# A two-layer Mamba/attention kernel on one core: unshifted write vectors moved through DRAM rows, score maxima turned on VectorE, and a newly searched instruction order

## The chip, the cores and the metric

The kernel runs on one core of a Trainium2 chip as one launch. The time is the device time of that core in microseconds, taken as the median of three runs. The engines are called by the profile's names: PE (TensorE), DVE (VectorE), ACT (ScalarE), POOL (GpSimd) and SP (SyncE, which issues nearly all the DMAs here).

## The reference, cut to what matters

`x` is 8 batches of 1024 tokens of 256 channels. Layer 0 is a selective scan with its feed-forward block and an MLP. Layer 1, the one whose computation the change touches, normalises `x` and adds an attention with a "line memory" and a second MLP:

```python
qkv = (x @ qkv_w + qkv_b).reshape(Bx, Tx, 3, H, DH)      # 16 heads of 16
attn = softmax(causal scores);  seq_out = attn @ v
x_prev = jnp.concatenate([jnp.zeros((Bx, 1, Dx)), x[:, :-1]], axis=1)
w1 = (x_prev @ w1_write).reshape(Bx, Tx, H, PD)           # PD = 4: 64 columns, of the token before
w2 = (x @ w2_write).reshape(Bx, Tx, H, PD)
write_lines, read_lines = exterior(w1, w2), exterior(x @ w1_read, x @ w2_read)
mem_score = sum over earlier tokens of decay**distance * (read_line . J write_line)**2
gated = mean over heads of sigmoid(mem_score * mem_scale) * sigmoid(x @ memg_w + memg_b)
out = (seq_out + gated * (x @ memv_w + memv_b)) @ out_w + out_b
```

The softmax needs the maximum of every row of scores. `w1` is a projection of the token before: row t of it is row t-1 of `x @ w1_write`, and row 0 is zero.

## The kernel before, in words

**Order.** The order of every engine's work is written at build time by a planner (`by_time`, fed by `layer0_tasks` and `layer1_tasks`). It knows for every task the engine (p = PE, a = ACT, v = DVE, g = POOL, s = SP), a length, a tick (when it is wanted), what must come before it, and how late its result is felt; it then takes tasks by time. `SHIFTS` moves the ticks of a kind of task, `DRIFT` and `PULL` weigh ticks against readiness, and `ACTIVE`, `WINDOW`, `LOW` are its model of PE's clock. Each engine runs its list strictly in order, so a wait holds all that is behind it on its engine. PSUM banks are given out by the same planner: pairs of banks for scores ("wide"), single banks for the rest ("dense").

**Layer 0** takes the first half of the span. PE adds scanned states and runs the projections, DVE scans, POOL forms the scans' inputs, and SP feeds broadcast rows.

**Layer 1** works batch by batch, 8 pairs of heads in each batch, 64 pairs in all. In a pair g:
- `sm` units (L1539): PE makes scores in nine pieces, DVE takes their row maxima into `smax` (L2131, L2134, L2138), 8 tiles of 128 rows for both heads.
- `mt` (L1547): one PE transpose of the 16 columns of `smax` into a dense bank, so that each row of 128 maxima lies in one partition. ACT writes the negated high part (`neg_hi`), DVE the rest (L2141, `neg_lo`).
- `maxima` on SP (L1343): two DMAs put them as extra rows of `qs`. Then the `st` units (L1557) make the transposed scores with the maximum already taken off, ACT exponentiates them, POOL masks the crossing tiles, `pv` (L1576) multiplies with the values, and `ot` (L1584) turns the result.

Once in a batch the dense work runs between the pairs: `xt` turns the normalised input into `xT`, `qk` (L1610) projects queries and keys, and for each of 8 token tiles there are
- `pa` (L1616): six matmuls of 464 columns (values, w1_read, w2_write, w2_read, the gate);
- `pb` (L1621 and L1624): six matmuls of 256 columns for `memv_w`, and six of 64 columns for `w1_write`, the latter with the weights side taken from `xT` one token earlier. `xT` has a leading column of zeros for that (the `zeros` task on DVE). ACT copies the 64 columns into `pt1[:, t % 4, 0:64]`.

As soon as a tile's `pb` is drained, POOL forms its outer products (`outer`, L2431) and DVE the lines (L2221). For each half batch of four tiles a chain follows: `square`, `length`, `unit`, `lt`, `jw`, `feat_r` and `feat_w` on POOL (L1166), `fw` and `fr` (L1642), scans on DVE, and `ms` (L1648). After the second `ms` of a batch SP may load the MLP's weights (L1290, L1293) over the buffers that the chain used. `e1` (L1668) and `e2` (L1673) add a rank-one term to these weights, then `f1` (L1681) and `o` (L1689), the MLP, can run, and the next batch's `pa` waits for its last `o`.

`pt1` and `pt2` hold four tiles, `outer` two. The `pa` of a tile is drained only when the `outer` of four tiles earlier is done.

Of the kernel before, what the change touches and what calls it, by code (L numbers as in the profile page):

```python
# [12 lines left out]
F32 = mybir.dt.float32  # L13
F32R = mybir.dt.float32r
BF16 = mybir.dt.bfloat16
ALU = mybir.AluOpType
# [3 lines left out]
P = 128  # L20
B, S, D = 8, 1024, 256
NT = S // P
# [429 lines left out]
LENGTH = {"xt": 0.44, "qk": 1.40, "pa": 1.28, "pb": 1.40, "lt": 0.44, "jw": 0.89, "fw": 0.44, "fr": 0.44, "ms": 0.44,  # L452
# [20 lines left out]
def layer1_tasks():  # L473
# [37 lines left out]
    def pair(g):  # L511

        b, first = g // NG, g * TICKS
        for n, unit in enumerate(MAX_UNITS):
# [3 lines left out]
                + (0.26 if n == len(MAX_UNITS) - 1 else 0), tick, ("p", "sm", g, n))  # L518
        place["mt", g] = first + TICKS - LEAD
        add("p", ("mt", g), 0.11, place["mt", g], ("v", "sm", g, len(MAX_UNITS) - 1))  # L520
        add("a", ("mt", g), EMPTY_A["mt"], place["mt", g], ("p", "mt", g), ("s", "maxima", g - 1) if g else None)
        add("v", ("mt", g), EMPTY_V["mt"], place["mt", g], ("a", "mt", g))
        add("s", ("maxima", g), 1.2, place["mt", g], ("v", "mt", g), late=2.0)
# [32 lines left out]
    for b in range(B):  # L556
# [19 lines left out]
        for c in range(NC):  # L576
            for t in range(TC * c, TC * (c + 1)):
# [3 lines left out]
                      a=[("g", "outer", (n - TC) // NT, (n - TC) % NT)] if n >= TC else [])  # L581
                dense(("pb", b, t), ("p", "pa", b, t))
                add("g", ("outer", b, t), 1.05, place["pb", b, t], ("a", "pb", b, t),
# [44 lines left out]
    for g in range(PAIRS):  # L628
# [7 lines left out]
          "pb": 0.62, "f1": 0.92}  # L636
# [14 lines left out]
def at_pace(used, start, length, active):  # L651

    now = start
    while length > 1e-9:
# [11 lines left out]
TURN, DRIFT = 0.1, 0.042  # L666
SHORT, RUN, STAY = 0, 1, 0
PULL = {"a": 0.01, "v": 0, "g": 0.01, "s": 0.0}
SHIFTS = {
    ("a", 0): {"xt": -23, "yt": 4, "res": 24, "skip": 19, "decay": 5, "gelu": 18, "dl": 8, "soft": 13, "cv": 1,  # L670
        "norm": 5.5, "m": -7, "silu_x": -9, "h": -10, "centre": -17, "o": -1, "shift": -2, "square": 8},
    ("a", 1): {"logistic": 56, "length": 41, "turn": -13, "deviation": 29, "f1": -26},
    ("g", 0): {"drive": 6, "du": 26, "join": 8, "offset": -15},
    ("g", 1): {"feat_r": 7, "select": 21},
# [5 lines left out]
    ("v", 0): {"scan": 44, "weigh": -49, "stats": 33.4},  # L680
    ("v", 1): {"gate": 34, "e2": 17, "wo": -6, "bias": 36, "pa": -2.4, "fw": 8, "stats": 7, "xt": 14, "lines": 59,
        "normal": 30, "zeros": 25, "sm": 3, "ot": -3},
}

# [6 lines left out]
def shift_of(name):  # L691

    attention = name[1] == "L1"
    return SHIFTS.get((name[0], int(attention)), {}).get(name[2] if attention else name[1], 0.0)
# [134 lines left out]
def pool_of(unit):  # L829

    if unit[0] != "L1":
        return "side" if unit[0] in LENGTH0 else None
    return "wide" if unit[1] in ("sm", "st", "ot") else "dense" if unit[1] in LENGTH or unit[1] == "mt" else None
# [24 lines left out]
def build(nc, x_in, w_in, p_in, moe1_in, moe2_in, resid, out):  # L858
    ctx = ExitStack()
    with ctx:  # L860
# [24 lines left out]
        def param(name):  # L885
# [33 lines left out]
        (qs, ks, exps, vals0, z0, parts, oT, rden, total, smax, smax2, gate_in, mem_in, gate8, l1_at) = place(  # L919
            arena_at, ("qs", [P, SLOTS, S], F32R), ("ks", [P, SLOTS, S], F32R), ("exps", [P, RING_COLS]),  # L920
            ("vals0", [P, vals_cols]), ("z0", [P, NT, D]), ("parts", [P, 2, 2, HALF], F32R), ("oT", [P, S]),
            ("rden", [P, NT, 2]), ("total", [P, NT, 2, VC1]), ("smax", [P, H, NT]), ("smax2", [P, 2, NT - TC, NC]),
# [253 lines left out]
        def _(sp):  # L1176
# [99 lines left out]
            def attention_task(task):  # L1276
# [62 lines left out]
                elif kind == "maxima":  # L1339
                    for who in "av":  # L1340
                        drained(sp, plan, ("mt", n), who)
# [1201 lines left out]
```

## Time and profile before

| | us |
|---|---|
| runs | 3705.8, 3708.39, 3709.55 |
| median | 3708.39 |
| the profiled execution's own time | 3712.95 |
| its span, first to last instruction | 3711.2 |
| PE busy | 3545.9 (96%) |
| DVE busy | 3105.8 (84%) |
| ACT busy | 2681.1 (72%) |
| POOL busy | 2286.7 (62%) |
| granted TensorE clock, mean | 0.985 |

Busy time is the union of an engine's instructions. PE's matmuls overlap, so for PE the distance between starts tells more than the duration of one. A granted clock of 1 is 2.4 GHz, and 0.5 is 1.2 GHz.

### The profile page before, as it was taken

Reading aid. Unit: us, or ns where it says so; the run is one execution under the profiler, and the core shown is the slowest. Engines: PE = TensorE matmul, PEld = TensorE weight load, DVE = VectorE, ACT = ScalarE, POOL = GpSimd, SP = SyncE. Lnnn points to the kernel's source line nnn. Section 1 sums busy time; section 2 is a strip of 40 time slices with the busy share of each in tenths; the row PEclk is TensorE's granted clock in tenths of the full one; section 3 lists DMA queues with packets and bytes.
Section 4 is the critical chain, followed back from the end, with each engine's and each line's share of the span. In section 5 each row is a group of like instructions: output and inputs, shape, how many; then the busy total and the mean of one; then the engine's idle time right before and its main releaser. Section 6 shows DMA issues by size and latency. Waiting matters only on the chain.

```text
span 3711.2 us, 63758 instructions
## 1 busy us (share of the span) xinstructions
PE 3545.9 (96%) x20578; PEld 2371.7 (64%) x20578; DVE 3105.8 (84%) x5827; ACT 2681.1 (72%) x4174; POOL 2286.7 (62%) x1799
## 2 busy tenths in 40 slices
PE   8999999999999999999897999999999999999998
PEld 4666666666666665666664766666666666767665
DVE  4788999999999999999957697786968778696873
ACT  7768878888888888888635667576675757667565
POOL 4787989999999999999914152331514233251421
PEclk9999999999999999999997999999999999999998
DMA  4445545455555555555523223232412323241230
GB/s 172 139 149 167 164 149 183 154 176 171 177 162 160 182 160 178 168 175 161 185 78 95 62 67 88 70 119 62 127 54 67 96 70 119 62 127 46 75 85 21
DMA packets 253342, 456.90 MB, mean 123 GB/s; under 512 B 26116, under 2 KB 80852, under 8 KB 250196
## 3 DMA queue, kind: packets, MB, share of 16 engines
q1 hardware_dynamic: 253012, 452.82, 39.5%
q8 instruction: 168, 2.75, 0.3%
q14 instruction: 162, 1.33, 0.1%
HBM read 381.07 MB, written 69.21 MB: 121 GB/s over the span
## 4 chain that ended last, share of the span: by engine, by line
PE 31%; DVE 12%; issue 4%; ACT 2%; POOL 1%; DMA 1%; SPq 0%; DVEq 0%; POOLq 0%; ACTq 0%
PE ps L1689 6%; PE ps L1576 4%; PE ps L1681 4%; PE ps L1557 3%; PE ps L1539 3%; DVE ps L2131 2%; DVE smax L2134 2%; PE ps L1610 2%; PE ps L1616 2%; PE ps L1621 1%; PE ps L1584 1%; ACT exps L1706 1%; DVE lines L2221 1%; PE ps L1624 1%; DMA g<-in_weights 1%
## 5 line engine op out<-in xcount | busy, mean ns | idle before, releaser
L2371 POOL TENSOR_TENSOR drive<-du,b_wide 128x1024 f32<-128x1024 f32 x512 | 1198.8, 2367 | 33.4 <-DVE ps L2108 24.5
L1706 ACT ACTIVATE ps<-delta,neg_a 128x512 f32<-128x512 f32 x1024 | 682.6, 685 | 145.4 <-DVE heavy L2086 109.1
L1706 ACT ACTIVATE exps<-ps 128x1024 f32<-128x1024 f32 (+1 forms) x640 | 598.7, 938 | 217.8 <-PE ps L1557 213.2
L2405 POOL TENSOR_SCALAR_AFFINE_SELECT exps<-exps 128x256 f32<-128x256 f32 x512 | 210.0, 424 | 798.0 <-ACT exps L1706 797.9
L2131 DVE CUSTOM_DVE_ANT_0 ps<-ps,later 128x512 f32<-128x512 f32 (+3 forms) x1024 | 474.6, 518 | 68.5 <-PE ps L1539 66.8
L1491 PEld LDWEIGHTS ps<-p_all,heavy 128*128 128x128 f32 x3072 | 352.9, 141 | 175.3 <-issue 84.1
L2086 DVE TENSOR_TENSOR heavy<-c_wide,ps 128x512 f32<-128x512 f32 x704 | 449.3, 674 | 11.8 <-issue 8.1
L2108 DVE TENSOR_TENSOR_SCAN ps<-ps,carry,drive 128x512 f32<-128x512 f32 x352 | 434.7, 1274 | 16.7 <-ACT ps L1706 15.3
L1491 PE MATMUL ps<-p_all,heavy 128*128 128x128 f32 x3072 | 413.7, 276 | 35.9 <-DVE heavy L2086 23.3
L2108 DVE TENSOR_TENSOR_SCAN ps<-ps,drive 128x512 f32<-128x512 f32 x352 | 413.2, 1213 | 31.9 <-ACT ps L1706 25.2
L2353 POOL TENSOR_TENSOR held<-held,c_wide 128x1024 f32<-128x1024 f32 x160 | 377.4, 2359 | 44.7 <-DVE held L2108 37.2
L2134 DVE TENSOR_REDUCE smax<-ps 128x2 f32<-128x1024 f32 x256 | 311.9, 1219 | 66.8 <-PE ps L1539 66.1
L1706 ACT ACT_TABLE_LOAD x277 | 355.4, 1283 | 5.7 <-PEq L2536 0.8
L1576 PE MATMUL ps<-exps,vals 128*32 128x512 f32 (+3 forms) x3072 | 306.6, 502 | 17.2 <-POOL exps L2405 8.0
L1557 PE MATMUL ps<-qs,ks 64*128 64x512 f32 (+3 forms) x1536 | 291.4, 405 | 11.8 <-DVE mem_in L2262 3.6
L1706 ACT ACTIVATE h<-ps,p_all 128x256 f32<-128x256 f32 (+1 forms) x384 | 193.8, 539 | 126.1 <-PE ps L1681 92.0
L1539 PE MATMUL ps<-ks,qs 64*128 64x512 f32 (+3 forms) x1536 | 262.3, 379 | 15.2 <-ACT exps L1706 10.9
L1427 PE MATMUL ps<-mT,w_up 128*128 128x512 f32 x512 | 244.7, 601 | 11.1 <-ACT h L1706 6.3
L1557 PEld LDWEIGHTS ps<-qs,ks 64*128 64x128 f32 x1536 | 137.0, 187 | 170.0 <-issue 78.2
L1689 PE MATMUL ps<-g,h 128*128 128x256 f32 x1024 | 236.0, 383 | 0.0
L1437 PE MATMUL ps<-w_down,h 128*128 128x256 f32 x1024 | 234.1, 382 | 0.0
L2108 DVE TENSOR_TENSOR_SCAN held<-ps,drive 128x512 f32<-128x512 f32 x160 | 189.7, 1208 | 49.9 <-POOL drive L2371 37.3
(219 smaller groups left out, 7151.4 us busy)
## 6 DMA issues: line engine op xcount, KB each, us to landing
b_wide<-bc_dram SPq DMA_DIRECT2D x512, 256.0 KB, 3.6
c_wide<-bc_dram SPq DMA_DIRECT2D x512, 256.0 KB, 3.6
stacks<-parts SPq DMA_DIRECT2D x192, 256.0 KB, 2.6
qs<-stacks SPq DMA_DIRECT2D x128, 192.0 KB
ks<-stacks SPq DMA_DIRECT2D x128, 192.0 KB, 4.3
x_row<-in_x SPq DMA_DIRECT2D x14, 1024.0 KB, 8.1
resid<-mix SPq DMA_DIRECT2D x9, 1024.0 KB, 5.4
x_row<-resid SPq DMA_DIRECT2D x9, 1024.0 KB, 5.5
```

The costliest lines, as they stand in the source:

```text
L1491: last = mm(acc_tile(t)[:, d * P:(d + 1) * P], heavy[:, slot, t * P:(t + 1) * P], ident, is_transpose=True, start=(u == 0 and d == 0 and t ...
L1539: last = mm(both[:, i * HALF + off:i * HALF + off + n], qs[head, slot, it * P:(it + 1) * P], ks[head, slot, ch * HALF:ch * HALF + n], star ...
L1557: last = mm(both[:, i * HALF + off:i * HALF + off + n], ks[head, slot, jt * P:(jt + 1) * P], qs[head, slot, at:at + n], start=True, stop=T ...
L1576: last = mm(ps[tile:tile + VP, PV_BANK, HALF - n:], vals[b % 2][:, first:first + VP], exps[:, at + i * apart + off:at + i * apart + off + ...
L1689: last = mm(bank[:, 0:D], h1[:, q % 2, m, tt * P:(tt + 1) * P], g2[:, m, :], start=(m == 0), stop=(m == MF - 1))
L1706: return nc.scalar.activation(out_, in_, func, **kw)
L2086: V.tensor_tensor(heavy[:, piece % W_SLOTS, :], c_wide[:, g % C_SLOTS, :], state_bank(k), ALU.mult).then_inc(weighed, 1)
L2108: V.tensor_tensor_scan(into, state_bank(k), drive[:, g % DRIVE_SLOTS, d, :], carry[:, e, n, d:d + 1] if j % NC else 0.0, ALU.mult, ALU.add ...
L2131: last = V.tensor_tensor_reduce(part[:, i, :], part[:, i, :], later[:, HALF - n:], 1.0, -3.0e38, ALU.add, ALU.max, into[:, i, :])
L2134: last = V.tensor_reduce(into[:, :, 0], part, AX_X, ALU.max)
L2353: G.tensor_tensor(states, states, wide(c_wide[:, g % C_SLOTS, :], MD), ALU.mult)\
L2371: G.tensor_tensor(drive[:, g % DRIVE_SLOTS, :, :], du[:, e, :, :], wide(b_wide[:, g % B_SLOTS, :], MD), ALU.mult).then_inc(driven, 1)
```

## The change

1. `pb` becomes six matmuls of 320 columns on the unshifted tokens. ACT copies the 64 columns into a new buffer `ahead` (8 tiles). When four tiles are there, SP writes them to rows 1 + token of a DRAM tensor `ahead_rows` (`put`: 128 partitions by 4 tiles, 256 bytes each), and then reads the rows one earlier back into `pt1` (`shift`: the same shape). Row 0 of each batch is set to zero once. `outer` waits for `shift`; all four of a half are released together.
2. `mt` leaves PE. `smax` becomes two slots of 32 columns (16 used, zeroed once on POOL); DVE turns one slot with four 32x32 transposes into `turned` (`flip`), ACT and DVE read `turned` instead of a PSUM bank.
3. The two memsets of `xT`'s leading columns go.
4. The planner's costs and edges follow, `DRIFT`, `PULL` and all of `SHIFTS` (layer 0's too) are new, and single units of `sm`, `st`, `pv` get shifts of their own (`UNIT_SHIFTS`). `LOW`, the edge of the planner's clock rule, has the same value in both files.

```diff
-"pb": 1.40
+"pb": 0.92
-        add("p", ("mt", g), 0.11, place["mt", g], ("v", "sm", g, len(MAX_UNITS) - 1))
+        add("v", ("flip", g), 0.42, at, ("v", "sm", g, len(MAX_UNITS) - 1), ("v", "mt", g - 1) if g else None)
+        add("v", ("mt", g), 0.45, at, ("a", "mt", g))
...
+                if t % TC == TC - 1:
+                    add("s", ("put", b, c), 0.45, place["pb", b, t], ("a", "pb", b, t), late=2.5)
+                    add("s", ("shift", b, c), 0.5, place["pb", b, t] + 1, ("s", "put", b, c),
+                        ("g", "outer", (n - TC) // NT, (n - TC) % NT) if n >= TC else None, late=2.9)
...
-TURN, DRIFT = 0.1, 0.042
+TURN, DRIFT = 0.1, 0.037
...
+                elif kind == "put":
+                    c = task[2]
+                    drained(sp, plan, ("pb", n, TC * c + TC - 1), "a")
...
+                    sp.dma_start(ahead_rows[n, 1 + c * HALF:1 + (c + 1) * HALF, :].rearrange("(t p) d -> p t d", p=P),
+                                 ahead[:, TC * c:TC * (c + 1), :]).then_inc(ahead_put, 16)
+                elif kind == "shift":
+                    c = task[2]
+                    sp.wait_ge(ahead_put, 16 * (NC * n + c + 2))
+                    if NC * n + c:
+                        sp.wait_ge(outer_done, TC * (NC * n + c))
+                    sp.dma_start(pt1[:, :, 0:64], ahead_rows[n, c * HALF:(c + 1) * HALF, :].rearrange("(t p) d -> p t d", p=P))\
+                      .then_inc(shifted, 16)
...
-                    for n, (k, by, of) in enumerate(three):
-                        mm(bank[:, 0:D], xT[of][:, k, tokens(t)], w[by][:, k, 0:D], start=(n == 0),
-                           stop=(n == len(three) - 1), skip_group_check=True)
-                    for n, (k, by, of) in enumerate(three):
-                        last = mm(bank[:, D:D + 64], xT[of][:, k, tokens(t, shift=0)], w[by][:, k, D:D + 64],
-                                  start=(n == 0), stop=(n == len(three) - 1), skip_group_check=True)
+                        last = mm(bank[:, 0:D + 64], xT[of][:, k, tokens(t)], w[by][:, k, :], start=(n == 0),
+                                  stop=(n == len(three) - 1))
...
+                elif kind == "flip":
+                    dve.wait_ge(maxed, g + 1)
+                    dve.wait_ge(neg_below, g)
+                    for at in range(0, P, 32):
+                        last = V.transpose(turned[:, at:at + 32], smax[at:at + 32, g % 2, :])
+                    last.then_inc(flipped, 1)
...
+                    pool.wait_ge(shifted, 16 * (NC * n + t // TC + 1))
```

## Rows read from the trace of the kernel before

**Rows 1.** The page: busy time by engine, and the granted clock in 40 slices

```profile
PE 3545.9 (96%) x20578; PEld 2371.7 (64%) x20578; DVE 3105.8 (84%) x5827; ACT 2681.1 (72%) x4174; POOL 2286.7 (62%) x1799
...
PEclk9999999999999999999997999999999999999998
```

**Rows 2.** Windows by stage: length, busy us (instructions), clock, DMA share, GB/s

```profile
1100.00:1740.00 640.00, 620.83 (x2931) 400.55 (x2929) 620.16 (x722) 540.77 (x862) 623.49 (x305) 1.00 0.55 169
1740.00:1900.00 160.00, 132.14 (x655) 97.40 (x654) 135.57 (x188) 91.71 (x143) 118.39 (x58) 0.89 0.45 146
1900.00:2100.00 200.00, 179.51 (x1083) 121.93 (x1083) 140.38 (x386) 111.55 (x164) 61.21 (x88) 0.89 0.27 76
2100.00:3640.00 1540.00, 1497.59 (x10742) 1041.10 (x10741) 1226.15 (x3318) 1005.90 (x1507) 514.18 (x847) 1.00 0.28 84
3640.00:3711.20 71.20, 54.38 (x345) 32.58 (x342) 20.68 (x58) 31.49 (x40) 13.23 (x29) 0.85 0.05 16
```

**Rows 3.** Windows of one batch: PE, PEld, DVE, ACT, POOL, clock, DMA

```profile
2355.00:2412.00 57.00, 55.97 (x420) 38.84 (x420) 50.94 (x145) 32.80 (x59) 29.75 (x44) 1.00 0.17 44
2412.00:2460.00 48.00, 45.60 (x326) 28.97 (x327) 45.16 (x110) 31.44 (x48) 23.11 (x36) 1.00 0.53 172
2460.00:2570.00 110.00, 107.45 (x766) 78.01 (x769) 75.89 (x215) 76.59 (x107) 19.93 (x42) 1.00 0.24 70
```

**Rows 4.** The chain in order of time, the same piece in two batches

```profile
2513.67 3.65 PE ps L1689 x16
...
2731.31 3.65 PE ps L1689 x16
```

**Rows 5.** The chain, 1895 to 2110: start, length, what; six matmuls each

```profile
1898.32 0.71 PE ps L1621 x6
1899.04 0.59 PE ps L1624 x6
...
1906.40 1.27 PE ps L1616 x6
```

**Rows 6.** Timeline of PE around two transposes of the maxima

```profile
2347.83 0.28 PE L1547 MATMUL ps<-p_all,smax 128*16 128x128 f32 x1
2347.94 3.62 PE L1689 MATMUL ps<-g,h 128*128 128x256 f32 x16
...
2699.76 0.27 PE L1547 MATMUL ps<-p_all,smax 128*16 128x128 f32 x1
2699.97 0.50 PE L1539 MATMUL ps<-ks,qs 64*128 64x512 f32 x2
```

**Rows 7.** Groups by form from 1900 on: the maxima transpose's weight load

```profile
L1547 PEld LDWEIGHTS ps<-p_all,smax 128*16 128x16 f32 x64 | 5.6, 88 | 13.8 <-DVE smax L2131 4.3 <-issue 4.0 <-ACT pt L1706 2.5
```

**Rows 8.** Groups by form from 1900 on: DVE's maxima work and short instructions

```profile
L2141 DVE SCALAR_TENSOR_TENSOR rows<-ps,rows 16x128 fp32r<-16x128 f32 x64 | 17.9, 280 | 4.7 <-ACT rows L1706 2.8
...
L2147 DVE COPY total<-ps 128x34 f32<-128x34 f32 x64 | 12.1, 189 | 32.2 <-PE ps L1584 32.2
...
L2245 DVE MEMSET gsum<- 112x1 f32 x24 | 1.4, 59 | 0.0
```

**Rows 9.** DMA issues from 1900 on: count, KB each, median us to landing

```profile
stacks<-parts SPq DMA_DIRECT2D x181, 256.0 KB, 2.6
...
ks<-stacks SPq DMA_DIRECT2D x128, 192.0 KB, 4.3
```

**Rows 10.** Timeline, one batch: last two outers, SP's weight load, first e1

```profile
2399.65 1.10 POOL L2431 TENSOR_TENSOR outer<-pt,pt 128x512 f32<-128x512 f32 x1
2410.77 1.09 POOL L2431 TENSOR_TENSOR outer<-pt,pt 128x512 f32<-128x512 f32 x1
...
2445.84 0.43 SPq L1293 DMA_DIRECT2D g<-in_weights  x1
...
2452.84 0.50 PE L1668 MATMUL ps<-rows 3*128 3x256 f32 x2
```

**Rows 11.** Timeline: SP issues a pair's maxima, PE begins that pair's st

```profile
2239.70 1.13 SPq L1343 DMA_DIRECT2D qs<-rows  x2
...
2246.33 0.40 PE L1557 MATMUL ps<-qs,ks 64*128 64x512 f32 x2
```

More of the change, by code:

```diff
@@ L580, in layer1_tasks @@
                       ("v", "gate", b - 1, NC - 1) if b else None, ("p", "zt", b - 2, NC - 1, KD - 1) if b > 1 else None,
[L581 to L583 removed]
+                      a=([("g", "outer", (n - TC) // NT, (n - TC) % NT)] if n >= TC else []))
+                dense(("pb", b, t), ("p", "pa", b, t), a=[("s", "put", b - 1, NC - 1)] if b else [])
+                if t % TC == TC - 1:
+                    add("s", ("put", b, c), 0.45, place["pb", b, t], ("a", "pb", b, t), late=2.5)
+                    add("s", ("shift", b, c), 0.5, place["pb", b, t] + 1, ("s", "put", b, c),
+                        ("g", "outer", (n - TC) // NT, (n - TC) % NT) if n >= TC else None, late=2.9)
+            for t in range(TC * c, TC * (c + 1)):
+                n = NT * b + t
+                add("g", ("outer", b, t), 1.05, place["pb", b, t], ("s", "shift", b, c),
                     ("v", "lines", (n - 2) // NT, (n - 2) % NT) if n >= 2 else None)
@@ L942, in build @@
         zero_rows = rows[80:82, 0, :]
-        pt1, pt2, outer, lines, norm, feat_w, feat_r, gsum, lines_at = place(
-            body_at, ("pt1", [P, TC, 2 * 4 * H]), ("pt2", [P, TC, 2 * 4 * H]), ("outer", [P, 2, 2 * H, 4, 4]),
+        pt1, pt2, ahead, none_ahead, outer, lines, norm, feat_w, feat_r, gsum, lines_at = place(
+            body_at, ("pt1", [P, TC, 2 * 4 * H]), ("pt2", [P, TC, 2 * 4 * H]), ("ahead", [P, NT, 64]), ("none_ahead", [P, 64]), ("outer", [P, 2, 2 * H, 4, 4]),
             ("lines", [P, 2, TC, 2 * H, 6]), ("norm", [P, TC * 2 * H]), ("feat_w", [P, TC, NPQ * H]),
@@ L1948, in attention_task @@
                 elif kind == "pb":
-                    f(pt1[:, task[2] % TC, 0:64], full(act, plan, task)[:, D:D + 64], ACT.Copy).then_inc(drained_a, 1)
+                    bank = full(act, plan, task)
+                    if n:
+                        act.wait_ge(ahead_put, 16 * (NC * n + 1))
+                    f(ahead[:, task[2], :], bank[:, D:D + 64], ACT.Copy).then_inc(drained_a, 1)
                 elif kind == "length":
@@ L2120, in attend @@
                     both = full(dve, plan, e).rearrange("p (i n) -> p i n", i=2)
+                    own = smax[:, g % 2, 0:2 * NT].rearrange("p (i t) -> p i t", i=2)
+                    if e[2] == 0 and g >= 2:
+                        dve.wait_ge(flipped, g - 1)
                     if g == 0 and e[2] == 0:
@@ L2127, in attend @@
                         part = both[:, :, off:off + n]
-                        into = smax[:, h:h + 2, it:it + 1] if it < TC else smax2[:, :, it - TC, ch:ch + 1]
+                        into = own[:, :, it:it + 1] if it < TC else smax2[:, :, it - TC, ch:ch + 1]
                         if it // TC == ch:
@@ L2155, in attention_task @@
                 kind, b = task[0], task[-1] if len(task) == 1 else task[1]
-                if kind in ("sm", "mt", "ot"):
+                if kind in ("sm", "flip", "mt", "ot"):
                     attend(task)
@@ L2161, in attention_task @@
                     drained(dve, L0_PLAN, ("dl", NH - 1, MI - 1), "a")
-                    for one in xT:
-                        V.memset(one[:, :, 0:1].bitcast(F32), 0.0).then_inc(setup1_v, 1)
                     V.tensor_tensor(param("outb"), param("outb"), param("gb2"), ALU.add).then_inc(setup1_v, 1)
@@ L2387, in attention_task @@
                     elif n == 1:
+                        G.memset(smax[:, :, :], 0.0)
                         ins = G.memset(later[:, 0:HALF - P], 0.0)
```

88 lines of the change are left out of this document (49 added, 39 removed), and 11 rows, old and new, of the table SHIFTS.

## The prediction

> **What bounds the kernel now.** I read the page's busy times and clock slices first [rows 1]. PE is busy 96% of the span, and its clock is full but for the start, the middle and the end. The windows by stage come next [rows 2]. In the last 640 us of steady layer 0, PE, DVE and POOL are all near 97% busy, so no single engine bounds it and the change takes no work out of it. In layer 1's steady stretch (2100 to 3640) PE is busy 1497.6 of 1540 us, idle only 42.4, at full clock; DVE has 1226 (80%), ACT 1006 (65%), POOL 514 (33%). Between the layers (1740 to 2100) the clock is at 0.89, and in the last 71 us at 0.85.
>
> The steady stretch repeats: the same piece of the MLP comes back 217.6 us later [rows 4]. Inside a batch the load is uneven [rows 3]. While pa, pb and the memory chain run (2355 to 2460, 105 us) PE is busy 101.6 and DVE 96.1, which is 92%. While the MLP runs (110 us), PE is busy 98% and DVE 69%. So PE bounds layer 1, with DVE close behind in half of each batch.
>
> **The change part by part.** The sum is made against the profiled execution, 3712.95 us with a span of 3711.2 and 1.75 around it. The median of the runs is 3708.39, which is 4.56 lower; I take the same difference off both.
>
> *pb.* Now a pb is six matmuls of 256 columns in 0.71 us and six of 64 in 0.59 us, 1.30 together; six of 464 columns take 1.27 us [rows 5]. Six of 320 lie between: (1.27 - 0.71) / 208 columns x 64 = 0.17, so 0.88. Each pb gives back 0.42 us of PE, and 64 of them 27 us. If 320 columns still cost what 256 do, it is 0.59 each, 38 us; if the step from 256 on is twice as steep, 0.25 each, 16 us. I take 27, since both neighbours are measured and 64 columns are a short way from one of them.
>
> The short matmuls are what decides this: in the row 64 columns cost 0.59 / 6 = 0.10 us each, nearly the 0.12 of 256 columns [rows 5]. The Trainium skill speaks against the saving: "VectorE: DVE Perf Modes", section "The TRN2 errata — SBUF-src ops pay a fixed extra latency per instruction", has a matmul at max(60, 6 + columns) cycles of 2.4 GHz, by which 64 columns cost 0.03 us, 256 cost 0.11 and 320 cost 0.14, an estimate of 0.01 us saved per pb and 1 us in all. By that the gain would be some 11 us in place of 37. The trace disagrees at its 64-column row by a factor of over three, and I go by the trace.
>
> *Transposes of maxima.* One costs PE 0.11 us from its start to the next unit's where a dense unit follows, and 0.21 where scores follow, since PE changes its kind of work twice [rows 6]. I take 0.16, so 64 give 10 us (7 to 13). PE's weight loader also idled 13.8 us ahead of them [rows 7]. Most of that will reappear before whichever unit comes next, so I count 0 of it and keep 13.8 as the upper end.
>
> *DVE.* It gets four 32x32 transposes per pair. No such row exists. A memset of one column takes 0.06 us and a copy of 34 columns 0.19 [rows 8], so four cost 0.24 to 0.76 us; nearer the copy, since 32 columns are read, less some overlap, I take 0.6, that is 38 us of DVE over layer 1. DVE's remaining maxima instruction (0.28 us) stays, now reading SBUF. That lifts DVE from 80% to some 84% in the steady stretch, and to about 95% in the memory part. It is hidden by PE as long as PE is the later of the two; without that cover it costs its 0.6 us per pair. ACT's copies are the same in number; pt's 64 columns only go elsewhere. The two memsets that go and the clearing of smax that comes are once each: nothing.
>
> The waits move too. The flip needs only DVE's own earlier results, so it holds nobody. ACT's copy of the maxima waits for the flip rather than for PE; behind it on ACT are the exponentials, behind DVE's mt are score units, as now. The chain loses one hop through PE and a bank.
>
> *put and shift.* 32 DMAs more on SP, and one for the zeros. The nearest rows are 256 KB to DRAM, landing after 2.6 us, and 192 KB from it in strides, 4.3 us [rows 9]; these are 128 KB each, in pieces of 256 bytes. A half batch so waits about 0.5 + 2.6 + 0.5 + 4.3 = 8 us (5 to 10) between its last pb and its first outer. The four outers, 1.1 us each, then run together, where now three are done before the last pb: 3.3 us more. So the chain to ms is up to 11 us longer. Where does that go? Now the last two outers of a batch start 11.1 us apart, with nothing but the pace of pb between them, and from the last to the weights' load are 35 us, with e1 7 us behind the issue [rows 10]: the second half's chain runs without slack, but the pbs ahead of it are spread out. An order that does them some 10 us earlier, with scores behind, covers the trip. I cost it at 0 for that, with 11 us a batch as the upper end.
>
> On SP, shift waits for put's landing, 2.6 us, and behind it are stack loads, saves and the maxima. The tightest pair in the steady stretch has its maxima issued at 2239.7 and its st begun at 2246.3, 6.6 us later [rows 11]; less about 2.6 for landing it can stand 4 us. So nothing here either.
>
> *The new order.* It touches everything, and the trace can only bound it. What it could recover: 42.4 us of idle PE in the steady stretch, and the low clock: 0.11 x 160 + 0.11 x 200 + 0.15 x 71 = 50 us [rows 2]. What it could lose is of the same kind; in layer 0 half a per cent either way is 9 us. I take 3 us of gain, between +15 and -25.
>
> **Sum.** -27 - 10 = -37 on PE. Not all is kept: in about 100 us between the layers PE waits on chains, and where DVE is at 95% freed PE time turns into waits. I keep five sixths: -31. With -3 for the order: -34. 3712.95 - 34 = 3679 for a profiled execution, and 3674 as the median.
>
> **The rivals.**
> 1. *The forecast*: 3674, its own range 3660 to 3690, chance 0.56. For it: PE idle 2.8% and full clock in 1540 us.
> 2. *The order does more*: a quarter of the 92 us of idle and low clock comes back, -20 more: 3654. For it, per-unit shifts are finer than before; against it, PE is already at 97%. Chance 0.18.
> 3. *DVE becomes the bound in the memory part*: all pbs lie in it, so their 27 us turn into waits, and only the transposes' 10 us less a few of the flips remain: 3700, within 3693 to 3706. For it 92% busy [rows 3], against it that scores can be moved into the MLP part, where DVE is at 69%. Chance 0.15, a third of which is no change that can be measured.
> 4. *The matmul formula holds*, short matmuls cost nearly nothing and pb gives nothing, only 10 us: 3698. The row's 0.59 us speaks against it (the page is the one named above). Chance 0.02.
> 5. *Slower: the memory chain is the bound*. Its place is between the last pb and e1. Of the 11 us more in each batch, 9 stay uncovered, because pa is held by pt1's four tiles until the first half's outers are done: 7 x 9 = 63, less 37, is +26: 3734. It decides from about 5.3 us per batch on (37 / 7). For it: no slack from outer to e1 [rows 10]. Against it: PE was busy in that very stretch with scores, and the first half can be brought forward. Chance 0.07, and another 0.02 for a smaller exposure that just eats the gain.
>
> That the change doesn't do what it says is hardly open: the matmuls and transposes are simply gone. Only "searched with the edge raised" may do nothing, which is case 1 as well.
>
> **How the numbers follow.** About 0.2% (7 us) is what a measurement of this kernel can tell from no change. Faster by more: cases 1, 2, two thirds of 3, and 4, together 0.86. Within it: a third of 3, with the small exposure of 5, 0.07. Slower: 0.07. The range runs from 3644, some way into case 2, to 3701, the middle of case 3; outside are the slow case, the worst of 3 and the best of 2, under 2 in 10.
>
> **What would show it right or wrong.** PE: 384 matmuls of 64 columns gone, and a row of six at 320 columns of 0.88 us in the chain; 64 transposes gone; the same MLP piece coming back after some 213 us. DVE: 64 x 4 transposes, 0.6 us per pair. DMA: the put landing in 2.6 us, the shift in about 4, the second half's pbs some 10 us earlier against ms. The forecast is wrong if the repeat stays at 217 us with PE idle over 5% in the memory part (case 3 if DVE is over 97% there, case 5 if PE waits for e1), or if clock slices fall below 1 in the steady stretch.

## The result and the profile after

The changed kernel takes 3740.71 us (median of 4, 3736.53 to 3745.15); the kernel before, on the same chip, takes 3707.10. The ratio is 1.0088 [1.0076, 1.0101]: 33 us slower, where 34 faster was forecast, and 40 us outside the range. All times are of undisturbed executions: one of e1's, at a granted clock of 0.74 and 4433 us, is left out. The profiled execution took 3739.64 us, with a span of 3737.8. Its page, lines as in [rows 1]:

```profile
PE 3555.4 (95%) x20130; PEld 2350.5 (63%) x20130; DVE 3177.8 (85%) x6081; ACT 2687.8 (72%) x4174; POOL 2302.0 (62%) x1800
...
PEclk9999999999999999999898999999999999999999
```

There are 448 matmuls fewer, and by the forecast 37 us of PE's time go with them, but PE is busy 9.5 us longer. Less work has taken more time. The windows by stage, as in [rows 2] (the last stretch ends with the span):

```profile
1740.00:1900.00 160.00, 137.17 (x657) 101.99 (x657) 134.52 (x191) 89.48 (x142) 113.93 (x57) 0.91 0.47 155
1900.00:2100.00 200.00, 179.57 (x1131) 123.12 (x1132) 153.88 (x414) 118.58 (x171) 61.40 (x93) 0.91 0.27 76
2100.00:3640.00 1540.00, 1475.90 (x10018) 993.45 (x10018) 1257.54 (x3465) 977.16 (x1462) 521.01 (x825) 0.97 0.29 84
...
3640.00:3738.00 98.00, 79.92 (x542) 49.82 (x541) 42.08 (x127) 51.79 (x66) 19.99 (x45) 0.91 0.11 29
```

The loss lies in the steady stretch: its clock is 0.97 instead of 1.00, and only 10,018 matmuls fit into it where 10,742 did. Of these 724, some 390 are those that the change takes out (56 a batch over 7 batches); the rest is lost pace. The part up to the first batch's end is better: its last `o` (L1714, before L1689) ends at 2109.2 us against 2133.9, so 25 us were won by then. From there each batch loses about 7: at the last `o` of batch 6 the changed kernel is 17 us behind, at that of batch 7 still 17, and what follows it costs another 9. The timeline rows of the first `e1` unit in batches 1 and 7 give the repeat, (3569.29 - 2221.14) / 6 = 224.7 us; the kernel before has 217.8 on the same six, and one of them, 217.6, is in [rows 4].

```profile
2221.14 0.49 PE L1693 MATMUL ps<-rows 3*128 3x256 f32 x2
...
3569.29 0.49 PE L1693 MATMUL ps<-rows 3*128 3x256 f32 x2
```

The windows of one batch, as in [rows 3], say where: the first 57 us, in which pa, pb and the second half's memory work lie.

```profile
2355.00:2412.00 57.00, 50.46 (x326) 31.45 (x330) 51.68 (x137) 32.25 (x51) 31.52 (x41) 0.92 0.25 67
2412.00:2460.00 48.00, 46.46 (x326) 31.15 (x319) 45.03 (x122) 27.77 (x48) 23.11 (x33) 0.98 0.49 160
2460.00:2570.00 110.00, 108.66 (x751) 75.31 (x751) 77.69 (x223) 78.03 (x105) 17.95 (x40) 1.00 0.23 60
```

PE is busy 50.5 of 57 us there, where it was busy 56.0, and at a clock of 0.92. Shorter windows around one place (same columns):

```profile
2395.00:2400.00 5.00, 4.81 (x31) 3.00 (x28) 4.94 (x8) 2.23 (x4) 4.52 (x5) 1.00 0.19 50
2400.00:2403.00 3.00, 0.42 (x6) 0.18 (x4) 3.00 (x6) 1.00 (x2) 2.76 (x3) 1.00 0.79 184
2403.00:2408.00 5.00, 3.39 (x20) 1.43 (x20) 4.74 (x13) 0.54 (x2) 4.92 (x6) 0.52 0.00 0
2408.00:2413.00 5.00, 4.94 (x26) 3.67 (x30) 2.07 (x9) 3.42 (x5) 1.31 (x3) 0.50 0.01 3
```

DVE and POOL are both busy almost without a break. PE is idle for 4.2 of 8 us (2400 to 2408). The granted clock goes from 2.4 to 1.2 GHz at 2403.2, after PE has been idle for 2.6 of 3 us, and stays there for about 10 us, the second wait included. PE's timeline there names what it waits for (idle time and releaser in brackets):

```profile
2402.95 0.57 PE L1575 MATMUL ps<-ks,qs 64*128 64x512 f32 x2 [2.58 <-DVE smax L2167]
2405.04 2.36 PE L1606 MATMUL ps<-exps,vals 128*32 128x512 f32 x16 [1.51 <-POOL exps L2443]
```

This comes back in each of batches 1 to 7, 225 us apart. Over the steady stretch PE's waits for that maximum of DVE are the largest (the view of PE's waits, 2100 to 3640: total, times, longest); before, the same pair of lines had 2.7 us.

```profile
PE ps L1575 <- DVE smax L2167: 22.9, 24, 3.1
PE ps L1606 <- POOL exps L2443: 8.2, 7, 1.5
```

Why is DVE late there? The timelines of DVE and of POOL:

```profile
2397.24 1.75 DVE L2258 TENSOR_TENSOR lines<-outer 128x96 f32<-128x96 f32 x3
...
2400.24 1.52 DVE L2258 TENSOR_TENSOR lines<-outer 128x96 f32<-128x96 f32 x3
2401.68 1.21 DVE L2167 TENSOR_REDUCE smax<-ps 128x2 f32<-128x1024 f32 x1
```

```profile
2395.21 2.15 POOL L2470 TENSOR_TENSOR outer<-pt,pt 128x512 f32<-128x512 f32 x2
2397.40 1.31 POOL L2477 TENSOR_TENSOR xn<-xn 112x512 f32<-112x512 f32 x1
2399.16 2.54 POOL L2470 TENSOR_TENSOR outer<-pt,pt 128x512 f32<-128x512 f32 x1 [0.45 <-DVE lines L2258]
2401.93 1.09 POOL L2470 TENSOR_TENSOR outer<-pt,pt 128x512 f32<-128x512 f32 x1 [0.24 <-DVE lines L2258]
2402.98 1.91 POOL L2443 TENSOR_SCALAR_AFFINE_SELECT exps<-exps 128x256 f32<-128x256 f32 x1
```

Three `lines` products take 1.75 and 1.52 us; three took 0.72 in the kernel before, with POOL idle for most of it (2400.53 on its timeline). And an outer of 1.1 us takes 2.54, and the select (L2443) for which PE waits the second time takes 1.91, where the same select takes 0.41 at 2392.79. The view of the line, before and then after (min/median/max in ns), shows the spread:

```profile
L2221 DVE TENSOR_TENSOR lines<-outer x192: 199/267/873, 1891.4 to 3501.7; 128x96 f32<-128x96 f32 x64, 128x64 f32<-128x64 f32 x64, 128x32 f32<-128x32 f32 x64
```

```profile
L2258 DVE TENSOR_TENSOR lines<-outer x192: 198/322/1398, 1894.1 to 3527.9; 128x96 f32<-128x96 f32 x64, 128x64 f32<-128x64 f32 x64, 128x32 f32<-128x32 f32 x64
```

Sorted by whether POOL ran during at least 0.3 of the instruction's time: before, 129 of them had POOL idle (mean 260 ns) and 63 had it busy (547); after, 55 (249) and 137 (551). Within each class a product costs the same as before, but more than twice as many now meet POOL at work. The four outers of a second half batch now start within 7 us (2395.21 to 2401.93), where they were spread over 26. This is how the new plan lays them. It is not the wait for the trip: in e10 below, without the trip, they stand at the same places and 135 products meet POOL. The plan was made with the trip in it, so what a plan made without it would do is not shown. The Trainium skill, "SBUF — State Buffer", section "SBUF: two separate sides", has DVE instructions with two SBUF inputs and GpSimd instructions that read SBUF share one pair of ports as an exclusive lock, which the one that starts first keeps for its whole instruction. The trace agrees: the second of the three products at 2397.24 alone takes 1.38 us and ends 0.14 us after POOL's `xn` does, and the outer at 2399.16, which starts 0.12 us behind a DVE scan of 1.28 us, is the one that takes 2.54.

The parts of the change itself read as follows. The chain of waits, one pa and one pb, as in [rows 5]:

```profile
1895.70 1.26 PE ps L1644 x6
1896.96 0.89 PE ps L1649 x6
```

The groups of the maxima's path (busy us, mean ns, idle before), as in [rows 7, 8]:

```profile
L2176 DVE STREAM_TRANSPOSE turned<-smax 32x32 f32<-32x32 f32 x256 | 50.5, 197 | 3.4
L2180 DVE SCALAR_TENSOR_TENSOR rows<-turned,rows 16x128 fp32r<-16x128 f32 x64 | 27.7, 432 | 8.5 <-ACT rows L1731 7.1
```

SP's timeline of one put and shift; the shift landed 2.2 us after its issue in the median, and the first outer began at 2395.21:

```profile
2389.47 0.38 SPq L1378 DMA_DIRECT2D ahead_rows<-ahead  x1
2392.68 0.38 SPq L1385 DMA_DIRECT2D pt<-ahead_rows  x1
```

### The profile page after: what moved, and what is told of

The parts are those of the page before. It is cut to its first block, busy times and chain, and to the rows that moved or that the text cites. A ratio compares the mean times of both kernels' runs of the same rounds, so it can differ in the third digit from the quotient of the medians.

```text
span 3737.8 us, 63121 instructions
## 1 busy us (share of the span) xinstructions
PE 3555.4 (95%) x20130; PEld 2350.5 (63%) x20130; DVE 3177.8 (85%) x6081; ACT 2687.8 (72%) x4174; POOL 2302.0 (62%) x1800
## 4 chain that ended last, share of the span: by engine, by line
PE 65%; DVE 17%; issue 6%; ACT 5%; POOL 4%; DMA 1%; SPq 0%; DVEq 0%; ACTq 0%; POOLq 0%
PE ps L1714 6%; PE ps L1527 6%; PE ps L1606 5%; PE ps L1706 5%; PE ps L1463 5%; PE ps L1427 4%; PE ps L1587 4%; PE ps L1575 4%; PE ps L1473 3%; DVE ps L2138 3%; DVE ps L2164 3%; PE ps L1538 3%; PE ps L1433 2%; PE ps L1420 2%; PE ps L1457 2%
## 5 line engine op out<-in xcount | busy, mean ns | idle before, releaser
L2443 POOL TENSOR_SCALAR_AFFINE_SELECT exps<-exps 128x256 f32<-128x256 f32 x512 | 217.6, 440 | 827.4 <-ACT exps L1731 826.9
L1606 PE MATMUL ps<-exps,vals 128*32 128x512 f32 (+3 forms) x3072 | 317.7, 518 | 15.7 <-POOL exps L2443 11.5
L1575 PE MATMUL ps<-ks,qs 64*128 64x512 f32 (+3 forms) x1536 | 272.0, 392 | 37.9 <-DVE smax L2167 23.1
L1714 PE MATMUL ps<-g,h 128*128 128x256 f32 x1024 | 235.6, 383 | 0.9 <-ACT exps L1731 0.9
L2138 DVE TENSOR_TENSOR_SCAN held<-ps,drive 128x512 f32<-128x512 f32 x160 | 188.7, 1208 | 50.5 <-POOL drive L2408 43.5
```

Source lines behind the costliest of these rows:

```text
L1575: last = mm(both[:, i * HALF + off:i * HALF + off + n], qs[head, slot, it * P:(it + 1) * P], ks[head, slot, ch * HALF:ch * HALF + n], star ...
L1606: last = mm(ps[tile:tile + VP, PV_BANK, HALF - n:], vals[b % 2][:, first:first + VP], exps[:, at + i * apart + off:at + i * apart + off + ...
L1714: last = mm(bank[:, 0:D], h1[:, q % 2, m, tt * P:(tt + 1) * P], g2[:, m, :], start=(m == 0), stop=(m == MF - 1))
L2138: V.tensor_tensor_scan(into, state_bank(k), drive[:, g % DRIVE_SLOTS, d, :], carry[:, e, n, d:d + 1] if j % NC else 0.0, ALU.mult, ALU.add ...
```

## The experiments

Three theories stood at first. *T* (the recorded texts call it D): the turns on DVE cost time, as PE does not cover DVE. *L*: the trip through DRAM lengthens the memory chain. *O* (there S): the new order itself loses. P in those texts is the forecast's own view, that PE's work sets the pace. "Old order" below means the planner's plan of the kernel before, "new order" that of the changed one.

**e1: no trip, new order.** ACT writes the unshifted 64 columns straight into pt1, so the write vectors are not moved by a token.

```diff
-                    f(ahead[:, task[2], :], bank[:, D:D + 64], ACT.Copy).then_inc(drained_a, 1)
+                    f(pt1[:, task[2] % TC, 0:64], bank[:, D:D + 64], ACT.Copy).then_inc(drained_a, 1)
...
-                    pool.wait_ge(shifted, 16 * (NC * n + t // TC + 1))
```

> The changed kernel in its own order, with put and shift left out: ACT writes the 64 columns straight into pt1 and outer waits for pb alone, so the write lines are those of the token itself (the shift by one token is left out of the computation). Theory L (the batch is a closed loop pa, outer, ms, weights, e1, MLP, pa; the trip lengthened it): outers start some 5 us earlier in each half, the low-clock stretch once a batch goes or shrinks, the repeat falls from 225 to some 218 us and the time from 3740 by 30 to 50 us. Rival S (the searched order is bad by itself, the trip is hidden): the repeat stays above 223 us and the time within 12 us of 3740.

Measured: 3740.71 us (median of three), 1.0086 [1.0064, 1.0108]; no trace of it is used. The time on the way through DRAM costs nothing in this order, within some 4 us. e10, which is e2 without the trip, agrees (3722.31 against 3722.58). Theory L falls, as far as it blames that time and not how the plan was laid for it.

**e2: turns left out, new order.** The four transposes are replaced by a memset of one column, so the maxima are not subtracted.

```diff
-                    for at in range(0, P, 32):
-                        last = V.transpose(turned[:, at:at + 32], smax[at:at + 32, g % 2, :])
+                    last = V.memset(turned[:, :] if g == 0 else turned[:, 0:1], 0.0)
```

> The changed kernel in its own order, the four 32x32 transposes of each pair replaced by a memset of one column (the maxima are left out of the softmax; its result is off only in rounding where scores are small, but it is not the reference's computation). A turn takes 4 x 0.197 us in the profile, some 0.6 us more than the memset. Theory D (DVE bounds the memory part): 64 x 0.6 = 38 us, nearly all of it comes back. Theory L: DVE's share matters only where the loop passes through it, 5 to 15 us.

Measured: 3722.58, 1.0044 [1.0028, 1.0061]. The turns cost 18 us, between what the two theories expected, and 15 stay.

**e3: only the turns on DVE, old order.** pb is as before (256 and 64 columns), PE's transposes go.

```diff
+ORDERS["p"] = [one for one in ORDERS["p"] if one[:2] != ("L1", "mt")]
+    ORDERS["v"].insert(ORDERS["v"].index(("L1", "sm", g, len(MAX_UNITS) - 1)) + 1, ("L1", "flip", g))
```

> The kernel before in its own order with one part of the change: the maxima are turned on DVE right after the last score piece of a pair, PE's transpose is taken out of the list, pb stays shifted in two lots. Theory P (PE's work sets the pace): 64 x 0.16 = 10 us faster. Theory L: 0 to 6 us faster, since the turn sits mostly where PE is filled with scores; with DVE at 92% in the memory part it may cost up to 10 us there.

Measured: 3739.82, 1.0085 [1.0069, 1.0101]: 32 us lost by this part alone, where either theory expected a gain or at most 10 us of loss.

**e4: e3 with pb in six matmuls of 320 columns, no trip** (the write vectors are not moved by a token).

> As the run before, and pb in six matmuls of 320 columns without any trip (the write lines are those of the token itself): all of PE's saving, none of the latency, in the old order. Theory P: 37 us of PE less, 31 us faster or more (3676). Theory L: PE's saving is on the loop only from pa to the last outer, 8 x 0.42 = 3.4 us a batch less what the old order's waits take back: 10 to 25 us faster.

Measured: 3734.72, 1.0072 [1.0055, 1.0089]. Next to the turns, 27 us less of PE work bring 5, less than either theory expected.

**e5: e3 with the transposes left out** (the memset of e2).

> As the run with the maxima turned on DVE in the old order, but a memset of one column stands in place of the four transposes (the maxima are left out of the softmax). All else of that part stays: PE has no transpose, ACT and DVE read SBUF. Theory D (the transposes' 4 x 0.2 us of DVE are what cost): back to 3708 or a few us under it, 3700 to 3712. Rival R (the restructuring costs: DVE's mt grew from 0.28 to 0.50 us, ACT's from 0.27 to 0.31, the hop is ordered otherwise): stays over 3725.

Measured: 3717.20, 1.0025 [1.0015, 1.0036]. Of e3's 32 us, 23 are the four transposes and 9 the rest of the new path, between what D and R expected. Some of that rest shows in the line view of the subtraction. Kernel before, where it reads PSUM and SBUF:

```profile
L2141 DVE SCALAR_TENSOR_TENSOR rows<-ps,rows x64: 279/280/282, 1937.0 to 3666.0; 16x128 fp32r<-16x128 f32 x64
```

e3, where both inputs are in SBUF:

```profile
L2175 DVE SCALAR_TENSOR_TENSOR rows<-turned,rows x64: 280/281/1070, 1935.5 to 3692.1; 16x128 fp32r<-16x128 f32 x64
```

One of its slow ones on e3's timeline, with what POOL does meanwhile:

```profile
2460.13 1.28 POOL L2446 TENSOR_TENSOR g_lo<-g_raw,g_hi 128x512 fp32r<-128x512 f32 x1 [5.13 <-ACT g_hi L1728]
...
2460.73 0.82 DVE L2175 SCALAR_TENSOR_TENSOR rows<-turned,rows 16x128 fp32r<-16x128 f32 x1
```

Sorted as above: with POOL idle 41 of them take 281 ns, with POOL busy 23 take 800. In the kernel before the two classes take 280 and 281. So the mean of 468 ns in e3's groups is no mean of like things: it is the port again.

**e6: the kernel before with four 32x32 transposes a pair into an unused tile.**

```diff
+                        for at in range(0, 128, 32):
+                            last = V.transpose(spare[:, at:at + 32], ident[at:at + 32, 0:32])
```

> The kernel before, unchanged but for four more 32x32 transposes on DVE behind each pair's last score piece, of constants into a buffer that nobody reads. Nobody waits for them; only DVE's time grows, by 64 x 0.8 = 51 us. Theory D: 20 to 30 us slower than 3708, in the steady stretch some 3 to 4 us a batch. Theory P (PE sets the pace, DVE is covered): within 5 us.

Measured: 3735.88, 1.0075 [1.0060, 1.0090]: 28 us slower. Nothing waits for them, so what costs is DVE's own time, some 51 us. This is theory T, shown in the untouched kernel. How it costs: PE's waits that grew in the steady stretch are for later DVE results, before and then e6 (the wait for `g_raw` has no row of its own before):

```profile
PE ps L1635 <- DVE parts L2199: 1.2, 7, 0.2
```

```profile
PE ps L1636 <- DVE parts L2204: 7.3, 7, 1.1
PE ps L1674 <- DVE g_raw L2284: 5.2, 7, 0.7
```

The idle time grows by 1.2 us a batch, and behind it 3.2 us a batch of clock are lost, where the kernel before loses none (the table below). The lost clock is the larger part.

**e7: the kernel before with the wide pb, no trip** (the write vectors are again not moved by a token).

> The kernel before with pb in six matmuls of 320 columns and no trip (write lines of the token itself); nothing else. 64 x 0.42 = 27 us less of PE. Theory P: 20 to 27 us faster. Theory D/L (the batch's loop passes through DVE and latencies, and PE fills): within 5 us of 3708.

Measured: 3692.91, 0.9959 [0.9944, 0.9973]: 15 us faster, of 27 us of PE time, between the two expectations.

**e8: the kernel before with pb's 64-column matmuls done twice.**

> The kernel before with the six 64-column matmuls of every pb done twice, the second time into a spare part of the bank: 64 x 0.6 = 38 us more of PE and nothing else. Theory P: 30 to 38 us slower. Theory D/L with slack on PE: under 10 us slower. If it costs all and the run without them gains nothing, the order is so tight that PE and DVE both are bounds.

Measured: 3744.51, 1.0107 [1.0082, 1.0131], 36 us. Added PE time is paid in full, removed PE time only half returned.

**e9: old order, wide pb, no trip, transposes left out. e10: the same in the new order.**

> The old order, write vectors 320 columns wide, no trip through DRAM, and the maxima's path over DVE without the four transposes (the rows then hold nothing of the maxima; the output is not the reference's). Theory 'PE and DVE bind together, the order is free of blame': e4's 3734.7 less the 22.6 us that the transposes cost between e3 and e5, 3712 us. To be set beside the same kernel in the new order (e10): their difference is what the new order does with the two parts' costs out of it. If the order is what loses, e9 is 10 us or more below e10.

> The new order with neither the trip nor the transposes. If both costs simply add (trip 0, transposes 18): 3723 us. If the trip was hidden only behind the DVE's transposes, it shows now: 3715 us or less. Against e9 it gives the order's own share: the rival that the new order gains (25 us in the transition, as its trace shows) says that e10 is at or below e9; the theory that it loses 7 us a batch says 10 or more above.

Measured: e9 3707.38, 0.9995 [0.9986, 1.0005]; e10 3722.31, 1.0046 [1.0030, 1.0062]. With both disputed costs out, the new order is 15 us slower than the old: theory O holds too. Their steady windows, e9 and then e10:

```profile
2100.00:3640.00 1540.00, 1471.63 (x10304) 1008.47 (x10301) 1245.73 (x3377) 1002.95 (x1499) 515.04 (x846) 0.99 0.28 83
```

```profile
2100.00:3640.00 1540.00, 1486.86 (x10176) 1005.11 (x10169) 1236.80 (x3346) 994.37 (x1484) 520.68 (x836) 0.98 0.28 82
```

e10 has PE busy longer, for fewer matmuls, at a lower clock: PE is not more idle, it is slower. POOL's outers stand in e10, without any trip, where they stand in the changed kernel:

```profile
2394.90 2.15 POOL L2468 TENSOR_TENSOR outer<-pt,pt 128x512 f32<-128x512 f32 x2
2398.79 2.56 POOL L2468 TENSOR_TENSOR outer<-pt,pt 128x512 f32<-128x512 f32 x1 [0.40 <-DVE lines L2257]
```

**e11: e3 with the turned block on partitions 32 to 63.**

```diff
-                        last = V.transpose(turned[:, at:at + 32], smax[at:at + 32, g % 2, :])
+                        last = V.transpose(turned[32:64, at:at + 32], smax[at:at + 32, g % 2, :])
```

> e3 (old order, only the maxima turned on DVE) with the turned block on partitions 32 to 63, where the rows that it is joined with start, in place of 0 to 31. If the subtraction's step from 280 to 468 ns comes from its two operands starting on different partitions, it falls back to about 300 ns and the run is about 8 us below e3's 3739.8, near 3732; if it comes from reading SBUF in place of PSUM whatever the partition, it stays at 468 ns and the time at 3740.

Measured: 3744.48, 1.0097 [1.0082, 1.0112]. It did not help: the start partition is not the cause. The mean of 468 ns had hidden two classes.

**e12: e3 with one transpose of 128x32 a pair.** It turns four 32x32 blocks in place; the copy and the subtraction run over 128x32, and eight small DMAs put the pieces where two did.

```diff
-                    for at in range(0, P, 32):
-                        last = V.transpose(turned[:, at:at + 32], smax[at:at + 32, g % 2, :])
+                    last = V.transpose(turned[:, :], smax[:, g % 2, :])
...
-                        sp.dma_start(qs[row:128:64, n % SLOTS, :].bitcast(F32).rearrange("h (i t) -> h i t", i=NT),
-                                     part.bitcast(F32)).then_inc(neg_in[n % SLOTS], 16)
+                        for q in range(4):
+                            sp.dma_start(qs[row:128:64, n % SLOTS, :].bitcast(F32)
+                                         .rearrange("h (i q t) -> h i q t", i=NT, q=4)[:, :, q, :],
+                                         part[32 * q:32 * q + 2 * NT, :].bitcast(F32)).then_inc(neg_in[n % SLOTS], 16)
```

> e3 with one transpose of 128x32 (each block of 32x32 in place) in place of four of 32x32, and the copy, the subtraction and eight small DMAs following in that shape. If the turns cost by their DVE time, 51 us fall to 13 to 20 and the subtraction to 0.2 us: 20 to 25 us less than e3, 3715 to 3720. If what costs is the longer chain from maximum to rows whatever its length (the copy waits for DVE and not for PE), it stays within 5 us of 3740. The eight DMAs could take some back on SP.

Measured: 3706.69, 0.9998 [0.9989, 1.0008], 33 us better than e3, more than expected. Its groups, as above:

```profile
L2176 DVE SCALAR_TENSOR_TENSOR neg<-turned,neg 128x32 fp32r<-128x32 f32 x64 | 19.6, 306 | 2.9 <-ACT neg L1730 2.7
L2172 DVE STREAM_TRANSPOSE turned<-smax 128x32 f32<-128x32 f32 x64 | 13.5, 212 | 2.2
```

Four blocks in one instruction take 0.21 us, one block alone 0.20. The Trainium skill, "VectorE: DVE Perf Modes", section "The three transpose paths", describes DVE's transpose as a grid of independent 32x32 blocks. By that one instruction does the work of four, where the rest of the path takes the blocks stacked; the trace agrees.

**e13 to e16: is the low clock the cause, or only a sign?** Theory C is that the fall of the clock costs the time, and D here that the wait does and the clock only shows it. e13 is the changed kernel with one PE unit just ahead of the 2.6 us wait done four times over. That lays more work into the gap. e14 also repeats the maximum's unit between the two waits. e15 is the changed kernel with e12's single transpose, e16 is e15 with e13.

```diff
-                    for tt in range(TC):
+                    for tt in list(range(TC)) * (4 if kind == "fr" and b and (c, ch) == (0, 2) else 1):
```

> The changed kernel with one unit a batch (the four 128x128 transposes of the last third of the written features of chunk 0, that stand just ahead of TensorE's 2.6 us wait for a maximum at 2400 us) done four times over: about 1.9 us more of TensorE work, laid into a gap of 4.1 us. Theory C (the changed kernel's loss is the granted clock, which falls to 0.5 for about 10 us after that gap once a batch, seven times; 39 us of clock lost in the steady part where the kernel before loses none): with the gap half filled the clock holds in most batches, the repeat falls from 224.8 towards 220 us, and the time from 3740 to between 3700 and 3720. Theory D (what costs is the waiting for VectorE itself and the clock only shows it): the added work costs 0 to 13 us, 3740 to 3753.

> As e13, and the maximum's unit between the two waits of the same gap done three times over (1.0 us more of TensorE work). Theory C: if e13's filling was too little the clock holds here, 3700 to 3720; if it was enough, this adds 0 to 7 us to e13. Theory D: 3745 to 3765.

> The changed kernel with one transpose of 128x32 a pair in place of four of 32x32, with the copy and the subtraction in that shape, as e12 did to e3. If VectorE's time for the turns costs here what it cost between e1 and e2 (20 us for 47 us of VectorE) and the subtraction's 0.2 us counts too: 3715 to 3722. The clock's fall once a batch should still be there, as it is in e2 and e10 without any transpose. If the shape of the eight small moves by SyncE matters in this order, where SyncE also carries the put and shift, it is above 3722.

> e15 and e13 together, with the whole computation in place. Theory C: both parts that lose are gone, the PE saving of 37 us and the transition's 25 us are left: 3680 to 3700, the first below the kernel before. Theory D: as e15, or up to 13 us above it, 3715 to 3735.

Measured: e13 3731.86, 1.0056 [1.0041, 1.0071]; e14 3732.18, 1.0042 [1.0022, 1.0061]; e15 3736.29, 1.0065 [1.0050, 1.0080]; e16 3733.01, 1.0057 [1.0042, 1.0072]. e13 does more work than the changed kernel in less time, with intervals that do not meet; that speaks against theory D. Of the seven places, the two at which the clock held in e13, the changed kernel first, then e13:

```profile
2625.00:2650.00 25.00, 21.78 (x111) 14.61 (x110) 20.31 (x50) 12.47 (x22) 13.41 (x17) 0.66 0.22 66
...
3075.00:3095.00 20.00, 17.40 (x92) 10.94 (x91) 17.70 (x47) 9.86 (x15) 11.78 (x13) 0.66 0.28 80
```

```profile
2625.00:2650.00 25.00, 21.34 (x156) 14.88 (x154) 24.53 (x68) 13.57 (x22) 15.01 (x21) 1.00 0.21 71
...
3075.00:3095.00 20.00, 18.48 (x124) 12.96 (x125) 19.56 (x55) 11.37 (x20) 10.98 (x15) 1.00 0.22 80
```

In the other five it still falls. Summed as (1 - clock) x length over windows at all seven, the lost clock is 39 us in the changed kernel and 17 in e13. The seven fillings are 7 x 1.3 = 9 us of PE (sixteen transposes took 1.96 us on the timeline and four 0.65; I had expected 1.9 more and not 1.3), laid into idle time. So theory C holds in its direction, but gave 9 us and not 20 to 40: five places still fall, and waits on POOL took part of the gap's place. e14, with more filling, lost only 12 us of clock in its trace and was no faster (its five times spread from 3718.65 to 3735.90). So the lost clock is not the whole loss, and a microsecond of it that comes back is not one of the kernel's time. PE's waits in e13's steady stretch, against the fence of the same view above:

```profile
PE ps L1575 <- DVE smax L2167: 11.5, 24, 1.3
PE ps L1606 <- POOL exps L2443: 9.4, 7, 1.7
PE ps L1673 <- POOL xn L2477: 5.9, 6, 1.4
```

e15 and e16 missed. In e16 the filling hardly held the clock: 31 us are lost in its trace against 34 in e15's, and the times can't be told apart, so e16 decides nothing on theory C. In e15, DVE is busy 41 us less in e15's steady stretch (1215.96 against 1257.54), yet only 4 us came. One wait there is new, and comes from the eight small DMAs:

```profile
PE ps L1589 <- DMA qs<-neg: 4.2, 6, 0.7
```

That, and a longer wait for the same POOL select (9.5 us, 8.2 in the changed kernel), is not the 14 us by which e15 lies above e2. Why the single transpose is worth 33 us in the old order and 4 in the new stays open.

**The books per batch.** The repeat is the mean of six, from the first `e1` unit of a batch to that of the next. PE's busy and idle shares of each kernel's steady window (2100 to 3640) are applied to it, and so is the clock lost in that window, (1 - clock) x length summed over the trace's records of the granted clock. All in us, each from one execution.

| kernel | repeat | PE busy | of it lost clock | PE idle |
|---|---|---|---|---|
| before | 217.8 | 211.8 | 0.0 | 6.0 |
| e7, wide pb | 216.3 | 208.5 | 0.0 | 7.7 |
| e6, DVE load | 221.5 | 214.4 | 3.2 | 7.2 |
| e3, turns | 221.7 | 213.2 | 1.7 | 8.4 |
| e12, one transpose | 217.2 | 210.4 | 0.0 | 6.9 |
| e9, old order | 218.6 | 208.9 | 1.2 | 9.7 |
| e10, new order | 221.8 | 214.2 | 4.7 | 7.7 |
| after | 224.7 | 215.3 | 5.7 | 9.4 |
| e13 | 223.4 | 214.5 | 2.5 | 8.9 |
| e14 | 223.0 | 214.1 | 1.7 | 8.9 |
| e15 | 224.7 | 214.8 | 5.0 | 9.9 |
| e16 | 225.0 | 215.6 | 4.5 | 9.4 |

After against before: PE work -4.6 (37 / 8, the forecast's saving), idle +3.4, clock +5.7, which leaves 2.4 us of busy time that I cannot name. Of it, 1.8 comes with the new order: e9 and e10 do the same work, and their busy time less the lost clock is 207.7 and 209.5. Why is not shown.

## Why the prediction was wrong

**The step that failed first** is "It is hidden by PE as long as PE is the later of the two", with DVE's 0.6 us a pair costed at 0. The size was off by a third (4 x 0.197 = 0.79 us against 0.6, just above my upper bound of 0.76), and DVE's share came out at 81.7% of the steady stretch; my own 38 us give 82%, not the 84% that I wrote. What failed is the cover. A window in which DVE is busy 80% says nothing of whether its time is hidden at each place: with both engines working through one fixed interleaving, what DVE does later PE waits for somewhere, and behind such waits the clock fell. e6 measures it, 28 us for 51 us of DVE: 1.2 us a batch more idle, 3.2 of clock. In the changed kernel the turns cost 18 (e2), in the old order 23 (e5).

**The subtraction** "stays, now reading SBUF" was costed at nothing. In e3 it meets POOL in 23 of 64 places and takes 800 ns; in the changed kernel in 28, and takes 626. It may be part of the 9 us by which e5 is slower than before; that it is all of it was not tried.

**pb** was right as PE work: 0.89 us against 0.88, and 3.3 us less busy per batch in e7, as 27 / 8. The Trainium skill's matmul rule ("VectorE: DVE Perf Modes", section "The TRN2 errata — SBUF-src ops pay a fixed extra latency per instruction") stood against it, with an estimate of 0.01 us saved per pb. The trace disagrees: 1.30 us became 0.89. But "I keep five sixths" failed: e7 keeps 15 of 27, and e4 beside the turns 5.

**The trip** was right: 0, by e1. From the put's issue to the first outer it took 5.7 us; 8 was forecast from the last pb on. Also right was that outers bunch, which I priced as a delay of 3.3 us. What bunching does to DVE was the miss: the lines then run beside POOL. And the bunching is in the new plan, with or without the trip (e10).

**The order**, -3 between +15 and -25, was +15 (e10 against e9), at the bound. It does gain early: the first batch's last `o` ends at 2113.1 us in e10 and at 2122.9 in e9, 10 us earlier. Of the rest of the changed kernel's 25, e9 has 11 over the kernel before, with the old order and less PE work. What it loses lies at the bunched outers, as a gap and as the clock behind it. The order was searched for the whole change, so +15 is its price without the turns and the trip. I had counted the clock only as something to win back. My own text named the sign, "if clock slices fall below 1 in the steady stretch", and gave it no price and no chance.

**The rivals.** Case 5 had the sign, but not the place: PE is idle ahead of the matmuls of the `e1` units for only 2.1 us in all of the steady stretch. Case 3 had the engine, but DVE is no more than 92% busy in the memory part (96.7 of 105 us), as before. No case had PE's clock falling; case 2 had it only as something to win back.

**By parts**, in the medians: the maxima's path without its transposes +9 (e5), the transposes +23 (e3 less e5), the wide pb -5 (e4 less e3), the new order with the trip +6 (changed kernel less e4): 33, which is what was measured. They are differences in one chain of kernels; in another chain the same part can cost something else (the turns 18 in the new order, the wide pb -15 without the turns). The last two are small because each is a sum: PE time saved against waits, and time won once, early, against what the batches lose.

No version here beats the kernel before with the whole computation in it; e12 equals it. e7's 15 us would need the trip in an order close to the old one, which was not tried; nor was a search of the order with POOL's effect on DVE in the planner's costs.

## What to carry to other kernels

Where two engines hand work back and forth in a fixed order, do not price an addition to the less busy one at nothing: here it cost between a third and a little over half of its time (e2, e5, e6). Put it into the untouched kernel as dead work and measure, as in e6. Before moving work together in time, look which of it slows the other and what PE will do meanwhile, since behind gaps of some 4 us here another 5.6 us of clock were lost a batch. And read the median beside the mean of a group before explaining it.

## What was not expected of the hardware

- A DVE instruction with two SBUF inputs (e3's subtraction, 16x128) took 281 ns with POOL idle and 800 with POOL busy; with one input in PSUM (the kernel before) 280 and 281.
- A DVE transpose costs the same 0.20 to 0.21 us for one 32x32 block and for four stacked on 128 partitions.
- At the place where PE was idle 4.2 of 8 us, once in each of seven batches, the granted clock fell to 0.5 for 7 to 17 us, and extra PE work in that gap made the kernel 9 us faster.
- PE work and time are not symmetric: 38 us more cost 36 (e8), 27 us less gave 15 (e7).
